# Queries, keys and values of a softmax layer as split products of rounded parts

## What is computed

```python
qkv = x @ W_qkv + b_qkv                      # x: layer-normed, W_qkv: 256 x 768
q, k, v = jnp.split(qkv, 3, axis=-1)         # 16 heads of 16
att = softmax(where(causal, q @ k.T * 0.25, -inf))
y = (att @ v) @ W_proj + b_proj
```

## Time and profile before

| | us |
|---|---|
| median of 3 runs | 4223.31 (4220.95 to 4225.34) |
| profiled execution | 4219.47 |
| its span | 4217.7 |
| PE busy in the span | 3914.6 (93%) |
| DVE, ACT, POOL busy | 2685.9, 2115.4, 1161.4 |

### The profile page before, as it was taken

The page is one execution under the profiler, slowest core; times in us unless marked ns, Lnnn a source line. Parts: engine busy times, 40 slices in busy tenths (PEclk is TensorE's granted clock), DMA queues, the critical chain, the costliest instruction groups (busy, mean ns, idle before and its releaser), DMA issues. The chain is left out here.

```text
span 4217.7 us, 74102 instructions
## 1 busy us (share of the span) xinstructions
PE 3914.6 (93%) x28420; PEld 2991.3 (71%) x28420; DVE 2685.9 (64%) x7775; ACT 2115.4 (50%) x3994; POOL 1161.4 (28%) x1097
## 2 busy tenths in 40 slices
PE   5999999999999899999999999999999699999992
PEld 2444444444445788888888888888888599999992
DVE  4788888888885566555565565555565555555555
ACT  1566666666665555554455554554454333333323
POOL 3233343343332311111112111121111133333334
PEclk8899999999998999999999999999999799999996
DMA  3543543444432100000000000000001133333336
GB/s 72 96 97 57 97 91 60 94 92 66 78 82 71 36 26 20 22 22 21 20 22 22 22 20 18 16 20 10 19 20 34 52 65 72 69 65 70 69 60 191
DMA packets 176466, 227.02 MB, mean 54 GB/s; under 512 B 27293, under 2 KB 152572, under 8 KB 176113
## 3 DMA queue, kind: packets, MB, share of 16 engines
q1 hardware_dynamic: 148080, 185.86, 19.2%
q0 software_dynamic: 26736, 31.70, 4.9%
q10 hardware_dynamic: 1296, 4.72, 0.3%
HBM read 90.63 MB, written 87.05 MB: 42 GB/s over the span
## 5 line engine op out<-in xcount | busy, mean ns | idle before, releaser
L861 ACT ACTIVATE probs<-a_scores 128x1024 f32<-128x1024 f32 (+3 forms) x768 | 615.0, 811 | 333.4 <-PE a_scores L757 327.7
L1014 DVE CUSTOM_DVE_ANT_0 a_scores<-a_scores,mask 128x384 f32<-128x384 f32 (+3 forms) x1024 | 480.3, 513 | 115.4 <-PE a_scores L743 109.7
L757 PEld LDWEIGHTS a_scores<-q_st,k_st 50*128 50x128 f32 x1536 | 147.2, 189 | 379.2 <-issue 242.8
L275 POOL TENSOR_TENSOR l_ln_rstd<-l_ln_ve,minus_half 128x4 f32<-128x4 f32 x80 | 81.9, 1023 | 1051.5 <-DVE l_ln_ve L248 1051.2
L1812 ACT ACTIVATE l_o<-l_num,l_den 128x64 f32<-128x64 f32 x960 | 222.1, 320 | 286.3 <-DVE l_den L2295 280.4
L1017 DVE TENSOR_REDUCE mx<-a_scores 128x2 f32<-128x1024 f32 x256 | 310.5, 1222 | 79.5 <-PE a_scores L743 78.3
L757 PE MATMUL a_scores<-q_st,k_st 50*128 50x512 f32 (+3 forms) x1536 | 345.3, 447 | 9.0 <-DVE mx L1014 4.3
L743 PE MATMUL a_scores<-k_st,q_st 48*128 48x512 f32 (+3 forms) x1536 | 303.9, 394 | 48.9 <-ACT probs L861 29.5
L777 PE MATMUL a_out<-probs,v_aug 128*32 128x512 f32 (+3 forms) x3072 | 344.2, 521 | 3.2 <-POOL probs L942 3.2
L942 POOL TENSOR_SCALAR_AFFINE_SELECT probs<-probs 128x512 f32<-128x512 f32 x256 | 164.7, 643 | 522.3 <-ACT probs L861 512.7
L2611 PE MATMUL e_out<-e_weights_hi,e_hT_hi 128*128 128x256 f32 x1088 | 303.9, 279 | 0.0
(11 more groups left out here) (266 smaller groups left out, 10388.8 us busy)
## 6 DMA issues: line engine op xcount, KB each, us to landing
q_st<-parts SPq DMA_DIRECT2D x192, 128.0 KB, 4.6
k_st<-parts SPq DMA_DIRECT2D x192, 128.0 KB, 6.5
expert_rows_scratch<-empty_row SPq DMA_DIRECT2D x34, 520.0 KB, 9.4
l_x<-x_scratch SPq DMA_DIRECT2D x32, 512.0 KB, 3.8
e_weights<-in_L_ffn_W_dram SPq DMA_DIRECT2D x16, 1024.0 KB, 7.0
e_rows<-expert_rows_scratch SPq DMA_DIRECT2D x24, 390.0 KB, 3.2
e_rows<-expert_rows_scratch SPq DMA_DIRECT2D x16, 520.0 KB, 3.9
x_in<-in_L_attn_x_dram SPq DMA_DIRECT2D x8, 1024.0 KB, 5.6
```

Of the source, the lines that this page charges most:

```text
L757: last = nc.tensor.matmul(psum_r[:, R.slot(u), h2, 0:w], k_st[rows, 2 * hg + pair, i * P:(i + 1) * P], q_st[rows, 2 * hg + pair, q0:q0 + w ...
L861: nc.scalar.activation(probs[:, k % 3, 2 * pair:2 * pair + 2, 0:w], psum_r[:, R.slot(u), :, 0:w], ACT.Exp).then_inc(R.evacuated[R.slot(u)], 1)
L1014: last = nc.vector.tensor_tensor_reduce(s, s, mask[:, HALF - w:HALF], 1.0, LEAST, ALU.add, ALU.max, out[:, h2, :])
```

## The change

1. In the softmax layer x and W_qkv are kept as two float32r parts, `hi` (rounded) and `lo` (the rest). Each float32 product becomes three: hi hi, lo hi, hi lo. A QK unit has 6 matmuls of 128x512 in place of 2, a V unit 12 of 128x256 in place of 4.
2. ScalarE still copies T1's bank, now to `xnT["hi"]`; then VectorE takes `lo` from the same bank, ahead of its other work of that step, and only that frees the bank.
3. In the first block one DMA brings all of W_qkv to `w_raw`; VectorE makes 18 copies (`hi`) and 18 subtractions (`lo`), where there were 16 copies.
4. A new SBUF map. With it go: SP loads Wf2 after the store of the last batch's x2, not after the last F unit; `high_late` of Wf2 goes from n = 4 to n = 6; GpSimd waits for the zeroing DMAs before it clears `l_state`; GpSimd's constants go from the stage's start to step 30 of the last turn, VectorE's two from there to step 14.

```diff
@@ first block
-            sp.dma_start(w_raw, w_view[:, :, 0:2 * D]).then_inc(load, 16)
-            sp.dma_start(w_qkv[:, :, 2 * D:3 * D], w_view[:, :, 2 * D:3 * D]).then_inc(load, 16)
+            sp.dma_start(w_raw, w_view).then_inc(load, 16)
...
             for c in range(CD):
                 for g in range(2 * 2 * HB):
                     cols = slice(g * 64, (g + 1) * 64)
-                    nc.vector.tensor_copy(
-                        w_qkv[:, c, cols].rearrange("p (h d r) -> p r h d", h=2, d=DH0),
-                        w_raw[:, c, cols].rearrange("p (r h d) -> p r h d", h=2, d=DH0)
-                        ).then_inc(filled, 1)
+                    nc.vector.tensor_copy(placed("hi", c, cols), given(c, cols)).then_inc(filled, 1)
+                nc.vector.tensor_copy(w_qkv["hi"][:, c, 2 * D:3 * D], w_raw[:, c, 2 * D:3 * D]
+                                      ).then_inc(filled, 1)
+            dve.wait_ge(filled, 7 + (4 * HB + 1) * CD)
+            for c in range(CD):
+                for g in range(2 * 2 * HB):
+                    cols = slice(g * 64, (g + 1) * 64)
+                    nc.vector.tensor_tensor(placed("lo", c, cols), given(c, cols),
+                                            placed("hi", c, cols).bitcast(F32), ALU.subtract).then_inc(filled, 1)
+                nc.vector.tensor_tensor(w_qkv["lo"][:, c, 2 * D:3 * D], w_raw[:, c, 2 * D:3 * D],
+                                        w_qkv["hi"][:, c, 2 * D:3 * D].bitcast(F32), ALU.subtract
+                                        ).then_inc(filled, 1)
@@ TensorE
             elif name == "QK":
                 m, qk, half = i // 4, i // 2 % 2, i % 2
-                for c in range(CD):
+                terms = [(c, a, x) for c in range(CD) for a, x in PRODUCTS]
+                for t, (c, a, x) in enumerate(terms):
                     last = nc.tensor.matmul(psum_g[:, :],
-                                            w_qkv[:, c, qk * D + m * P:qk * D + (m + 1) * P],
-                                            xnT[:, c, half * HALF:(half + 1) * HALF],
-                                            start=(c == 0), stop=(c == CD - 1))
+                                            w_qkv[a][:, c, qk * D + m * P:qk * D + (m + 1) * P],
+                                            xnT[x][:, c, half * HALF:(half + 1) * HALF],
+                                            start=(t == 0), stop=(t == len(terms) - 1))
             elif name == "V":
-                last = two_tiles(i, xnT, w_qkv[:, :, 2 * D:3 * D])
+                last = two_tiles_split(i, xnT, {part: w_qkv[part][:, :, 2 * D:3 * D] for part in w_qkv})
@@ ScalarE
                 if name == "T1":
-                    last = nc.scalar.copy(xnT[:, c, half * HALF:(half + 1) * HALF], psum_g[:, :])
+                    nc.scalar.copy(xnT["hi"][:, c, half * HALF:(half + 1) * HALF], psum_g[:, :]
+                                   ).then_inc(turned_hi, 1)
+                    return
@@ VectorE
+        def low_turned(b, i):
+            dve.wait_ge(turned_hi, b * 4 + i + 1)
+            at = (slice(None), i % CD, slice(i // CD * HALF, (i // CD + 1) * HALF))
+            nc.vector.tensor_tensor(xnT["lo"][at], psum_g[:, :], xnT["hi"][at].bitcast(F32),
+                                    ALU.subtract).then_inc(G.evacuated[0], 1)
...
-        ON_DVE = ("OUT", "END", "N", "P", "V")
+        ON_DVE = ("OUT", "END", "N", "P", "V", "T1")
@@ linear layer, SP
-                wait_products()
+                store_last()
                 load_late(1, raw_f[1], Wf2)
-                store_last()
                 load_late(2, raw_f[0], Wf1)
@@ linear layer, VectorE
-                        if first and n == 4:
+                        if first and n == 6:
                             high_late(1, raw_f[1], wf2, 32)
```

More of the change, by code:

```diff
@@ L328, in softmax_layer @@
     x_in = sb("x_in", [P, TT, D])
-    xnT = sb("xnT", [P, CD, T])
+    xnT = {part: sb(f"xnT_{part}", [P, CD, T], F32R) for part in ("hi", "lo")}
     parts = sb("parts", [P, 2, 2, T], F32R)
     v_new = sb("v_new", [P, TT, D])
-    w_qkv = sb("w_qkv", [P, CD, 3 * D])
+    w_qkv = {part: sb(f"w_qkv_{part}", [P, CD, 3 * D], F32R) for part in ("hi", "lo")}
+    PRODUCTS = (("hi", "hi"), ("lo", "hi"), ("hi", "lo"))
     bias_v = sb("bias_v", [P, D])
@@ L394, in _ @@
                                      allow_slow_non_contiguous=True).then_inc(load, 16)
-            sp.wait_ge(load, 16 * (8 + 8 * HB))
+            sp.wait_ge(load, 16 * (7 + 8 * HB))
         @block.vector
@@ L416, in _, with placed, given @@
             ln_h.sum_third(dve, 0, chain_h)
-            dve.wait_ge(load, 16 * (8 + 8 * HB))
+            dve.wait_ge(load, 16 * (7 + 8 * HB))
             nc.vector.tensor_scalar(bias_qk[:, 0:HB], bias_qk[:, 0:HB], SCALE, None,
                                     ALU.mult).then_inc(filled, 1)
+            def placed(part, c, cols):
+                return w_qkv[part][:, c, cols].rearrange("p (h d r) -> p r h d", h=2, d=DH0)
+            def given(c, cols):
+                return w_raw[:, c, cols].rearrange("p (r h d) -> p r h d", h=2, d=DH0)
             for c in range(CD):
@@ L460, in _ @@
         def _(pe):
-            pe.wait_ge(load, 16 * (8 + 8 * HB))
+            pe.wait_ge(load, 16 * (7 + 8 * HB))
             for c in range(CD):
@@ L688, in two_tiles, with two_tiles_split @@
                                             start=(c == 0), stop=(c == CD - 1))
+            return last
+        def two_tiles_split(i, lhs, rhs):
+            for jj in range(2):
+                j = 2 * i + jj
+                terms = [(c, a, w) for c in range(CD) for a, w in PRODUCTS]
+                for t, (c, a, w) in enumerate(terms):
+                    last = nc.tensor.matmul(psum_g[:, jj * D:(jj + 1) * D],
+                                            lhs[a][:, c, j * P:(j + 1) * P], rhs[w][:, c, :],
+                                            start=(t == 0), stop=(t == len(terms) - 1))
             return last
@@ L1152, in before @@
         def before():
+            for i in range(4):
+                low_turned(0, i)
             for i in range(4):
@@ L1284, in linear_layer @@
         ln1 = LayerNorm(nc, sb, sem, "l_ln1", G4, 2, minus_half, on_act=True)
-        sb = after(HEADS_AT)
         x2 = sb("l_x2", [P, G4, D])
@@ L1289, in linear_layer, with split_place @@
         a3 = sb("l_a3", [P, 2, G4, D])
[L1290 to L1297 removed]
+        def split_place(name, shape, other_name, other_shape):
+            part = sb(name, shape, F32R)
+            return part, at(sb.start, other_name, other_shape)
+        wo = {"hi": sb("l_wo_hi", [P, ME, D], F32R)}
+        wo["lo"], raw_o = split_place("l_wo_lo", [P, ME, D], "l_wo_raw", [P, ME, D])
+        hT = {}
+        hT["hi"], qT = split_place("l_hT_hi", [P, MF, HALF], "l_qT", [P, NP, HALF])
+        hT["lo"], kT = split_place("l_hT_lo", [P, MF, HALF], "l_kT", [P, NP, HALF])
+        o = sb("l_o", [P, 2, E1])
+        rows = sb("l_rows", [P, G4, RW])
+        nT1_lo = at(sb.start, "l_nT1_lo", [P, CD, HALF], F32R)
         v_aug = sb("l_v", [P, G4, H1, DV])
         kt = sb("l_k", [P, G4, E1])
[L1300 removed]
+        nT2_lo = at(sb.start, "l_nT2_lo", [P, CD, HALF], F32R)
+        assert sb.free <= TAIL_AT
+        sb = after(TAIL_AT)
+        wf1 = {"hi": sb("l_wf1_hi", [P, CD, DF], F32R)}
+        wf1["lo"], raw_f1 = split_place("l_wf1_lo", [P, CD, DF], "l_wf1_raw", [P, CD, DF])
+        wf2 = {"hi": sb("l_wf2_hi", [P, MF, D], F32R)}
+        wf2["lo"], raw_f2 = split_place("l_wf2_lo", [P, MF, D], "l_wf2_raw", [P, MF, D])
+        raw_f = (raw_f1, raw_f2)
+        assert sb.free <= END_AT
+        sb = after(END_AT)
+        scores = sb("l_scores_kept", [P, 2, 2, 4, P])
+        nT2 = at(END_AT + 4096, "l_nT2", [P, CD, HALF])
+        nT2_hi = at(END_AT + 4096, "l_nT2_hi", [P, CD, HALF], F32R)
+        state = sb("l_state", [P, NP, 2 * DV])
+        nT1 = {"hi": sb("l_nT1_hi", [P, CD, HALF], F32R), "lo": nT1_lo}
         lg = sb("l_logits", [P, G4, E])
```

95 lines of the change are left out of this document (38 added, 57 removed).

## The result

In the first comparison, on one chip, the changed kernel took 4211.59 us (median of 20 runs) against 4224.62 (20 runs) before: ratio 0.9973, 95% interval 0.9963 to 0.9983, so 11.4 us less. That is half of the 22.5 us forecast. In two later comparisons the same kernel stood at 1.0002 (0.9989 to 1.0016) and 0.9976 (0.9962 to 0.9990). The mean of the three ratios is 0.9984, some 7 us. Over all runs the medians are 4212.8 (44 runs) and 4223.3 (121 runs), 10.5 apart. The change makes the kernel faster, by a third to a half of the forecast.

A forecast was written before the change was run, and what follows sets the result against it. TensorE was taken as the bound, though not in each step (busy 115.49 of 120 us). -30.8 + 3.4 + 3.0 + 0 - 2.6 + 4.5 = -22.5 from 4219.47 gave 4197.0; with medians 3.8 higher, 4201 us, range 4189 to 4214.

The forecast's parts named there:

- the sign: Whole kernel: predicted faster with chance 0.78, same 0.15, slower 0.07.
- the 4.4 us kept per turn: Turns with a next batch: 4.4 us saved each (2.5 to 5.3), -30.8 over seven turns.
- The units: QK and V units of a turn: 1.46 and 1.48 us each, saving 0.45 and 0.43, 5.3 a turn.
- The lost 0.65: Ahead of V 0 and V 2, waits for VectorE take back 0.45 of QK 3's saving and 0.2 of V 2's.
- VectorE's low part: Four VectorE subtractions of 0.69 us a turn, at the T1 units: cost 0.3 per turn (0 to 1.8).
- The falls: Around the T1 units TensorE's clock falls once per turn, costing 1.4 us, and this comes back each turn.
- slower by the clock: Rival, chance 0.07: shorter QK and V steps let the clock fall in three more places a turn, 4.2 us lost; 4232.
- The first turn: One of the seven turns, each forecast to keep 4.4 us.
- The start: First block +3.4 us, T1 in before() +3.0 (0.75 per unit), QK 0 to 3 there 0, QK 4 to 7 -2.6.
- The -2.6 in that for QK 4 to 7: QK 4 to 7 between the first maxima: gapless, two at half clock and two at full, saving 2.6 us (1.5 to 3).
- The late loads: Tail: Wf2 loads after x2's store and lands later, VectorE and TensorE wait; +4.5 us (2 to 8).

The follow-up runs named there:

- the padded kernel: Changed kernel with one useless matmul ahead of each QK unit and two in each V unit, making units as long as before: 4242.62 us, ratio 1.0061.
- two moves in its start and tail: Changed kernel, low-weight subtractions between first transposes and late weights rounded at n = 10 and 12: 4201.69 us; the same on GpSimd's split of turned norms: 4218.26.
- filled start: Changed kernel with useless matmuls in TensorE's idle time in before(), 30 ahead of the first maxima and some ahead of later scores: 4219.79 us, ratio 1.0003.

## Why the prediction was wrong

The mechanism and the sign were right. The step that failed is the 4.4 us kept per turn, the largest term of the sum. Over the 18 turns the changed kernel saved 157.03 - 154.31 = 2.7 a turn: 16 us in six turns where 26 were forecast. Of the 1.7 missing, 1.0 is the size of the units, and 0.7 is the clock, which had no term. By the prediction's steps:

- **The units** are the term that was mis-sized most. "I add 0.06 for the switch from one kind of matmul to the next" was 0.19. The earlier trace rows have starts within a run of one kind, which leaves out entering and leaving it, while the 1.91 that it was taken from had them in. Each QK and V unit saved 0.30 to 0.34 us, not 0.45 and 0.43: over 12 units 3.8 a turn in place of 5.3.
- **The lost 0.65** was lost elsewhere. QK 3 and V 2 kept their 0.3 each. "VectorE has no gap" was read from rows without an idle time, but a small operation there carries a wait in its duration: L254 on 128x8 took 0.52 at 638.96 of the trace before and 0.28 at 643.99 after, and both times it ended within 0.03 us of a GpSimd operation of 1.04 us. "In the steps of the other ten VectorE idles for longer" failed at N 4, two steps behind QK 7: TensorE's wait there went from 0.30 to 0.75. So 3.4 of the 3.8 are kept, and 157.03 - 153.62 = 3.4 is what a turn with the short fall shows.
- **VectorE's low part**, taken as 0.3 a turn out of 0 to 1.8, was about right by itself. With a short fall it costs nothing, without one 0.66, which is what the prediction had in "the new subtractions use up what a higher clock would give back". Cutting it gave 2.6 to 4.2 us over seven turns, 0.4 to 0.6 a turn.
- **The falls** were taken as one of 1.4 us in each turn for ever, the same before and after. The short one costs 0.9 where the subtraction is cut. A long one costs 4.4 to 5.9, and the changed kernel has some, before none in 12 turns. The subtraction alone in the kernel before brought two of them in six turns. That is the rival "slower by the clock", in part: mostly in how long the old fall at T1 lasts, and in two turns of 18 at V 0, among the units where it was put. (Its 4232 leaves out the 0.2 that a turn keeps in it; with 7 x 0.2 it is 4230.)
- **The first turn** should have given 4.4. From N 0 to N 4 it took 148.7 and 152.7 in two profiles before, 157.9, 148.0 and 147.9 in three after: that is anything from -5 to +9, the longest stretch at half clock in it being 41 and 44 us before, and 68, 44 and 48 after.
- **The start** was right: T1 +3.4 (forecast +3.4), four T1 units 0.72 more each (0.75). N 0 came at 95.1 and 94.1 before, 96.7, 100.3 and 99.7 after, 4.3 later by the means, where the forecast had 3.8. The -2.6 in that for QK 4 to 7 rests on a misread row: they were neither gapless nor two at half clock, as QK 5 took 2.43 us in all, and QK 6 and 7 waited 0.34 and 0.41 for ScalarE.
- **The late loads** were right: 4.4 us where the rounding was moved away, 5.3 where the tail's part was put into the kernel before (forecast 4.5), with VectorE waiting 5.65 and 6.12 (forecast 6).

The Trainium skill, TensorE: Matmul & The Clock Gate, section "HAM oscillation — how this bites in real kernels", spoke for the clock rival: idle gaps between bursts let the clock fall back. The trace agrees in part: the falls in the turns begin at such gaps, though the section's gaps are waits for a DMA and these are of 0.9 and 1.1 us. But the same gap of 0.9 us also stands in turns without any fall. The filled and the padded kernel show the other side: more matmuls didn't bring a higher mean clock.

What stays open: why the clock stays low for 17 to 20 us in some turns, 3.4 in others and not at all in most, and why the padded units lowered it further. The runs show where it happens and what it costs, not the condition; that the subtraction makes long falls more frequent is likely, but 18 turns against 12 don't prove it.

## What to carry to other kernels

Price a group of matmuls from the last instruction before it to the first behind it, and take the new one's entry from a row of the same kind of group: intervals within a run leave 0.19 us per unit out, here 1.5 us a turn. Where each turn of a profile shows the same clock fall, don't take its length as fixed when a change touches the waits there: here it went from 3.4 us to none or to 17 and 20, and the range should hold both. When all units get shorter, look for the next place where another engine is just in time, as N 4 here. And small costs outside the loop are worth undoing after such a change: two moves in its start and tail gave 8 and 11 us in two comparisons, about as much as the new products.

## What the runs showed of the hardware

- One kernel on one chip differs by some 20 us from run to run, with the granted clock: over 100 runs of before with clocks from 0.962 to 0.975 (one more, at 0.923, left out) the time changes by 2.8 us for 0.001 of mean clock, and the mean of the changed kernel's 44 runs is 0.9657, before's 0.9676. So the kernel before stood at 4215.4 (23 runs) and 4226.1 (29 runs) in two comparisons on the same chip, 10.7 apart, as much as the change gives.
- At an equal mean clock the changed kernel lies 13.2, 12.6 and 14.0 us below before in the three comparisons, an estimate from the line through those 100 runs. This is why 0.9973, 1.0002 and 0.9976 can belong to one kernel. The 0.0019 of mean clock that it loses takes 5 us of it back.
- Added matmuls didn't raise the mean clock: it was 0.9627 with padded units, lower than the 0.9653 beside it, and 0.9651 with the filled start, where the changed kernel had 0.9653 to 0.9660.
- A small VectorE operation can last as long as the GpSimd operation beside it: L254 on 128x8 takes 0.17 us by itself, and 0.28, 0.52 and 1.28 where it meets one, each time ending with it. No idle time is shown for that.
- The same wait of 0.90 to 0.92 us of TensorE at the T1 units stands in turns where the clock stays at 2.4 GHz, where it falls for 3.4 us, and where it falls for 17 or 20.
- A group of float32r matmuls of 128x512 costs 0.19 us beyond its intervals whether it has 2 or 6 matmuls.
